# Issuing the four Q and K loads of a batch one behind the other's landing

## Reference

```python
xn = _layernorm(x)
# layer 0 attention: 16 heads of 8 features, window of 128 tokens to each side, not causal
qkv = einsum('btd,ed->bte', xn, w_in) + b_in
q, k, v = split(qkv, 3)                      # each (8, 16 heads, 512, 8)
scores = einsum('bhqd,bhkd->bhqk', q, k) / sqrt(8)
scores = where(|i - j| <= 128, scores, -1e30)
ctx = einsum('bhqk,bhkd->bhqd', softmax(scores), v)
attn = xn + ctx @ w_out.T + b_out
# layer 0 ffn: rows of xn quantized to int8, times int8 weights, scaled, plus bias
x = x + attn + ffn(xn)
# layer 1: softmax attention over 512 tokens of a batch with one head of 128,
# and 8 experts of which each token takes 2, on layernorm(x)
x = x + attn1(layernorm(x)) + moe(layernorm(x))
```

## Time and profile before

| | |
|---|---|
| median of three executions | 546.78 us |
| profiled execution | 549.95 us |
| its span | 548.2 us |
| TensorE busy | 476.5 us (87%) |
| VectorE busy | 407.4 us (74%) |
| ScalarE busy | 343.2 us (63%) |
| GpSimd busy | 306.2 us (56%) |
| mean granted TensorE clock | 0.958 of full |
| loads of Qs from parts_dram (14) | 384.0 KB each, median 5.9 us from issue to landing |
| loads of Ks from parts_dram (14) | 384.0 KB each, median 9.0 us from issue to landing |

### The profile page before, as it was taken

How to read it: one execution, slowest core, us unless ns; L and a number is a source line. 1 busy time by engine, 2 the same in 40 slices (tenths; PEclk the granted TensorE clock), 3 DMA queues, 4 the chain that set the end, 5 groups by cost and what they waited for, 6 DMA issues and landing times. The chain is left out here.

```text
span 548.2 us, 17188 instructions
## 1 busy us (share of the span) xinstructions
PE 476.5 (87%) x5963; PEld 317.3 (58%) x5963; DVE 407.4 (74%) x1508; ACT 343.2 (63%) x870; POOL 306.2 (56%) x361
## 2 busy tenths in 40 slices
PE   6178798998898989988988998799999899999991
PEld 5135344454454444544544455576676799999991
DVE  6788768878788788787876824597888877576762
ACT  2071667777777776767775775577875655555550
POOL 5681672645655836656502022377777777777673
PEclk9675989999999999999998999999999999999996
DMA  3866228258274483571750111531113333445562
GB/s 79 209 146 114 63 60 176 66 137 156 55 181 104 109 176 84 138 157 31 178 107 21 42 43 59 204 124 53 51 55 94 89 93 109 137 148 155 178 176 93
DMA packets 51382, 61.00 MB, mean 111 GB/s; under 512 B 10002, under 2 KB 42134, under 8 KB 49697
## 3 DMA queue, kind: packets, MB, share of 16 engines
q1 hardware_dynamic: 45824, 50.26, 37.9%
q0 software_dynamic: 4320, 8.47, 4.4%
q10 hardware_dynamic: 1152, 1.18, 0.7%
HBM read 31.68 MB, written 28.39 MB: 110 GB/s over the span
## 5 line engine op out<-in xcount | busy, mean ns | idle before, releaser
L722 DVE CUSTOM_DVE_ANT_0 A<-A,band 128x320 f32<-128x320 f32 x256 | 123.5, 499 | 28.0 <-PE A L908 27.7
L908 PE MATMUL A<-Ks,Qs 48*64 48x320 bf16 (+2 forms) x1024 | 111.3, 300 | 18.8 <-DVE mneg L722 9.9
L946 PE MATMUL SB<-Qs,Ks 50*64 50x320 bf16 (+2 forms) x1024 | 123.5, 292 | 3.9 <-ACT Pb L564 3.2
L567 ACT ACTIVATE Pb<-SB 128x320 f32<-128x320 f32 x256 | 96.5, 442 | 37.8 <-PE SB L960 36.3
L908 PEld LDWEIGHTS A<-Ks,Qs 48*64 48x64 bf16 x1024 | 46.5, 108 | 92.9 <-DVE mneg L722 40.8
L717 DVE TENSOR_REDUCE mneg<-A 128x2 f32<-128x384 f32 (+1 forms) x128 | 79.5, 621 | 25.9 <-PE A L916 25.7
L1922 POOL DMA_INDIRECT results<-y,xt x71 | 75.0, 1057 | 28.5 <-issue 24.7
L973 PE MATMUL PV<-Pb,Va 128*32 128x320 f32 (+2 forms) x1024 | 86.0, 408 | 5.5 <-ACT Pb L564 4.5
L564 ACT ACTIVATE Pb<-SB 128x384 f32<-128x384 f32 (+1 forms) x128 | 66.2, 545 | 39.0 <-PE SB L960 38.9
L960 PE MATMUL SB<-ends,ident 64*64 64x128 bf16 x768 | 83.4, 219 | 0.0
L1299 POOL DMA_INDIRECT expert_rows<-pay,pos x64 | 62.2, 972 | 31.7 <-issue 18.8
(11 more groups left out here) (273 smaller groups left out, 920.2 us busy)
## 6 DMA issues: line engine op xcount, KB each, us to landing
Qs<-parts_dram SPq DMA_DIRECT2D x14, 384.0 KB, 5.9
Ks<-parts_dram SPq DMA_DIRECT2D x14, 384.0 KB, 9.0
xt<-expert_rows SPq DMA_DIRECT2D x71, 65.0 KB, 1.9
yb<-results SPq DMA_DIRECT2D x7, 512.0 KB, 4.3
parts_dram<-qp SPq DMA_DIRECT2D x16, 192.0 KB, 2.8
parts_dram<-kp SPq DMA_DIRECT2D x14, 192.0 KB, 2.8
xb<-in_x SPq DMA_DIRECT2D x8, 256.0 KB, 3.2
parts_dram<-qp SPq DMA_DIRECT2D x16, 128.0 KB, 2.7
```

The lines of the kernel that those rows point to most:

```text
L567: act.activation(Pb[:, group % 4, c, 0:w], bank[:, 0:w], ACT.Exp).then_inc(act_exp, 1)
L722: nc.vector.tensor_tensor_reduce(bank[:, 0:w], bank[:, 0:w], band[:, skip:skip + w], -1.0, 3e38, ALU.add, ALU.min, mneg[:, step % 2, first ...
L908: mm = nc.tensor.matmul(bank[out:out + HP, at:at + w], Qs[b % RING][rows, a, HP * sub:HP * sub + HP], Ks[b % RING][rows, a, lo:lo + w], st ...
L946: nc.tensor.matmul(out[r0:r0 + HP, at:at + w], Ks[b % RING][rows, a, HP * sub:HP * sub + HP], Qs[b % RING][rows, a, lo:lo + w], start=not ...
```

## The change

SyncE waits ahead of each load of `load(g)` until all loads in front of it on `dma_stack` have landed. For the first of a batch that is 64 times g, which the batch before has long reached; for the second, third and fourth it is the landing of the load just issued. `load_first` is as it was.

```diff
                 sp.wait_ge(stored, PARTS * (g + 1))
                 for par in range(2):
                     r0 = HP * par
+                    sp.wait_ge(dma_stack, LOADS * g + 16 * (2 * which + par))
                     sp.dma_start(tile[pg][r0:r0 + MROW].rearrange("r a t -> r (a t)"),
                                  parts_dram[g, which, par].rearrange("n (d a) t -> (n d) (a t)", a=NA))\
                         .then_inc(dma_stack, 16)
```

## The result

The changed kernel takes 600.89 us (median of 4, 600.17 to 601.52) against 547.2 us for the kernel before: a ratio of 1.0967, 95% interval 1.0934 to 1.1000. The forecast was 589.5 us within 566 to 612. The profiled execution took 601.42 us, with a span of 599.7 us, 51.5 us more than before. All lines of the kernel from L266 on have moved down by one.

A forecast was written before the change was run, and what follows sets the result against it. Layer 0 is bound by the chain from issued loads through the last landing to TensorE's piece at slot 16; 10.4 us at batch 2, 30.5 over five periods and 1.7 at the end make 42.6, so 589.5 us (566 to 612).

The forecast's parts named there:

- What bounds layer 0: TensorE's piece at slot 16 waits for the last of four loads, which already land just in time, with no slack.
- L: Time from issue to landing of a load alone in SyncE's queue: 4.2 us taken, four in a row 16.8 us.
- The three-piece sum: Estimate for a lone load: 1.0 us before data flows, 2.4 of flow, 0.6 to the landing, 4.0 us in all.
- Batch 1: In the prologue, GpSimd waits for base2's store behind the later loads: 4.9 us, carried to batch 2's loads at 92.0.
- Batch 2's piece: TensorE's piece at slot 16 starts at 108.8 in place of 98.43, a shift of 10.4 us.
- The period: Layer 0, piece to piece, batches 3 to 7: 16.8 + 24.4 + 1.7 = 42.9 us against 36.8, five times 6.1 more.
- The idle time before: TensorE idle time at L908 ending with a landing: 5.4 us in 7 places, to grow to some 30 to 40.
- The clock: TensorE's clock falls behind each stall, costing 1.7 us a period and 1.7 once more behind batch 7's.
- SyncE's queue behind the loads: Store of base2, load of base_r and place_max cost nothing: fourth issue 12.6 us behind the first, placing 16.4.
- Quick lone loads: Rival at the loads: a lone load takes 3.4 us, four 13.6, a period 39.0; 563 us; chance 0.15.
- The clock that stays down: Rival on TensorE: low clock after each stall costs 4.7 in place of 1.7 us; 607 us; chance 0.13.
- The case of no loss: Rival at slot 16's piece: overlap worth nothing, a lone load takes 2.9 us, 4 us gained, 543 us; chance 0.05.

The follow-up runs named there:

- two in flight: The changed kernel, but each K load waits only for the Q load two places in front: 547.19 us, ratio 0.9977 against the kernel before.
- pairs: The changed kernel with one wait per batch left, between the Q pair and the K pair of loads: 565.89 us, ratio 1.0314 against the kernel before.
- serial halves: The changed kernel with each load cut into two 192 KB halves, every half waiting for the one in front: 639.84 us, ratio 1.1661 against the kernel before.
- the moved store: First store of base2 put ahead of batch 1's loads: in the changed kernel 598.54 us, ratio 1.0905; in the kernel before 546.06 us, ratio 0.9966.
- the eight chained halves: Changed kernel, early base2 store, eight chained half loads, first step's columns first; the piece waits for four: 593.3 us, ratio 1.0838 against the kernel before.
- a chain that lands nearly in time: Eight half loads with early base2 store, only the first step's four chained: 547.78 us, ratio 1.0001; the same without waits between loads 0.9924.

## Why the prediction was right, step by step

**What bounds layer 0** was right: S, the time from the first issue to the fourth landing, sets the batch. Four kernels with S of 12.1, 13.8, 18.3 and 23.4 us (two in flight, pairs, the change, serial halves) took 547, 566, 601 and 640 us. The sum was too small, though: 42.6 us said, 51.5 between the two spans and 53.7 between the medians. The traces show where: 1.2 us more at batch 2's piece, 8.5 more in the five periods, 1.0 less at the end.

**L** was the mis-sized term: 4.2 us taken, 4.5 measured (4.1 to 5.1). The three-piece sum took 2.4 us of flow from the spacing of overlapped landings; a lone load flows for 3.1. The fixed part was nearly right, 1.4 against 1.6. The measured 4.5 lies between that sum and the first of four, 4.9 us: followers do seem to slow the first, but only by some 0.4 us, less than I argued from the bytes moved before its landing. S became 18.25 us on average in place of 16.8.

**Batch 1** was right in size: GpSimd's wait 20.78 us (near 21 said), batch 2's loads at 91.79 (92.0 said). Of the path the prediction had only one half, and that the size came out so well is partly luck. TensorE's own wait for batch 1's loads, 2.92 us, was not priced and lies close behind GpSimd's: the moved store gives back only 2.8 of the 4.7 us, and with the store out of the way in both kernels the change still puts batch 2's loads 4.9 us later (89.01 against 84.10).

**Batch 2's piece** came at 110.04, 11.6 us late against 10.4.

**The period** is (333.13 - 110.04) / 5 = 44.6 us against 42.9: S explains 1.45 of the difference, the stretch from a piece to the next loads the rest (26.4 against 24.4 + 1.7 = 26.1). Five times 7.8 us in place of 6.1 are 39 us in place of 30.5. The shift at batch 7's piece is 333.13 - 282.36 = 50.8 us; 0.7 more come behind it, where 1.7 was said.

**The idle time before** was misread: the 5.4 us in 7 places are four landings, three of them counted twice, on TensorE (2.2 us) and on its weight loads (3.2 us). No term of the sum hung on it; the 30 to 40 us that it was to become are 42.9.

**The clock** was right as a mechanism and in size: low behind every stall, 2.0 us a period by the 26.4 and 24.4. It was 0.50 for 6.4 us behind batch 4's stall, longer than the row taken from before.

**SyncE's queue behind the loads**, costed at nothing, was right for the change: place_max is issued at 161.65, 25.5 us after batch 3's first load, with the fourth issue long past. The cover was thinner than the text said, though: the eight chained halves, whose last issue comes some 21 us behind the first, lost 31 us there.

**The rivals.** Quick lone loads (563 us) fall by L. The clock that stays down (607 us) was nearest in time, but the runs show the stall and not the clock as the greater part. The case of no loss falls by L above 3.06. The Trainium skill's "DMA: Bandwidth & Descriptors" (section "Anatomy of one DMA") gives about 2.0 us plus the bytes over 436 GB/s for transfers issued from GpSimd; the 2.9 us estimated by it were taken for loads that SyncE issues, of which that section does not speak. Measured are 4.5 us, by the halves 1.4 fixed and 3.1 of flow, where that formula would have 2.0 and an estimated 0.9.

## What to carry to other kernels

Price a chained transfer near what the first of an overlapped group takes from issue to landing (4.9 us for a true 4.5 here), not from the spacing of landings, and set the sum against the time from the first issue to the consumer's wait: here 12.1 us were there and 18.25 were used, every batch. Two transfers in flight were as good as four, and a chain that lands nearly in time cost under 1%; so look at the slack of the consumer and at what stands behind the waiting instruction, rather than at the number of waits. Just-in-time loads are a place to gain, too: with a wait for the first half of the columns alone, no idle time ended with a landing any more.

## What the runs showed of the hardware beside this

A lone load of 384 KB to 48 partitions took 4.5 us, by estimate 1.4 us and 3.1 us of flow (127 GB/s); with four in the queue one landed each 2.4 us (164 GB/s). Issuing half of them from a second queue changed nothing. And TensorE kept busy with idle matmuls through its stalls took back 9.5 us of 53.7.
